# Softmax sums of an attention kernel: folded over 32 partitions on VectorE, finished by narrow matmuls, inverted in 16 columns

## The reference, cut to what matters

```python
x = query                                   # (4, 2048, 512) float32
xn = layernorm(x)                           # over the last axis
q, k, v = heads(xn @ q_w.T + q_b), heads(xn @ k_w.T + k_b), heads(xn @ v_w.T + v_b)   # 16 heads of 32
attn = softmax(q @ k.T / sqrt(32))          # 2048 x 2048 a head, 4 x 16 heads
y = tanh(xn @ weight @ aux1 @ aux2 + bias)
out = x + (attn @ v) @ out_w.T + out_b + y
```

## Time and profile before

| | us |
|---|---|
| median of 3 runs | 4175.6 (4172.01 to 4176.85) |
| span of the profiled execution | 4167.9 |
| PE, POOL, DVE, ACT busy | 4078.0, 3253.1, 3127.0, 2356.4 |
| issue of the merge to its landing, median | 10.4 |

### The profile page before, as it was taken

The page is one execution under the profiler, slowest core; times in us unless marked ns, Lnnn a source line. Parts: engine busy times, 40 slices in busy tenths (PEclk is TensorE's granted clock), DMA queues, the critical chain, the costliest instruction groups (busy, mean ns, idle before and its releaser), DMA issues.

```text
span 4167.9 us, 77711 instructions
## 1 busy us (share of the span) xinstructions
PE 4078.0 (98%) x21216; PEld 2490.3 (60%) x21216; DVE 3127.0 (75%) x5058; ACT 2356.4 (57%) x4515; POOL 3253.1 (78%) x1180
## 2 busy tenths in 40 slices
PE   8999999889999999999999999999999999999999
PEld 6888888645555555555555555555555555555467
DVE  4443334668888888888888888888888888888454
ACT  2221222157676666666676666666666767666621
POOL 1222222179999999999999999999999999999930
PEclk9999999999999999999999999999999999999999
DMA  4444445368878888888888888878888888888787
GB/s 169 162 161 160 151 160 166 122 141 174 172 165 176 176 175 176 171 172 175 173 174 178 177 170 173 171 168 175 176 177 173 175 172 171 176 176 174 154 260 263
DMA packets 246352, 722.11 MB, mean 173 GB/s; under 512 B 87392, under 2 KB 88416, under 8 KB 184544
## 3 DMA queue, kind: packets, MB, share of 16 engines
q0 software_dynamic: 55296, 402.68, 49.8%
q1 hardware_dynamic: 107648, 201.88, 14.2%
q10 hardware_dynamic: 83040, 113.01, 9.8%
HBM read 178.00 MB, written 136.31 MB: 75 GB/s over the span
## 4 chain that ended last, share of the span: by engine, by line
PE 53%; DMA 14%; issue 7%; ACT 3%; POOL 2%; ACTq 0%; POOLq 0%; SPq 0%; DVE 0%; DVEq 0%
PE sm_bank L948 16%; PE st_bank L964 16%; PE pv_bank L970 16%; DMA dma_sum<-pool_sum 10%; DMA dma_sum<-probs 3%; ACT probs L781 3%; PE sm_bank L235 3%; PE sm_bank L970 1%; POOL pool_sum L716 1%; PE st_bank L235 1%; POOL ctx_out L741 0%; DMA q_stack<-s_y 0%; PE sm_bank L957 0%; DMA q_stack<-max_row 0%; POOL dma_sum L727 0%
## 5 line engine op out<-in xcount | busy, mean ns | idle before, releaser
L862 DVE TENSOR_REDUCE part_max<-sm_bank 128x1 f32<-128x512 f32 x4016 | 2442.3, 678 | 412.3 <-PE sm_bank L948 406.0
L716 POOL TENSOR_TENSOR pool_sum<-pool_sum,probs 128x2048 f32<-128x2048 f32 x512 | 2504.9, 4892 | 16.7 <-ACT probs L781 0.9
L781 ACT ACTIVATE probs<-st_bank 128x512 f32<-128x512 f32 x3840 | 1959.4, 616 | 608.6 <-PE st_bank L964 580.6
L964 PE MATMUL st_bank<-q_stack,k_stack 97*128 97x512 f32 x4096 | 1648.4, 403 | 19.2 <-ACT probs L781 8.3
L948 PE MATMUL sm_bank<-k_stack,q_stack 96*128 96x512 f32 x4016 | 1655.1, 412 | 3.0 <-issue 2.7
L948 PEld LDWEIGHTS sm_bank<-k_stack,q_stack 96*128 96x128 f32 x4016 | 763.3, 190 | 550.7 <-DVE part_max L862 334.1
L964 PEld LDWEIGHTS st_bank<-q_stack,k_stack 97*128 97x128 f32 x4096 | 779.9, 191 | 274.8 <-ACT probs L781 128.0
L970 PE MATMUL pv_bank<-probs,v_pair 128*32 128x512 f32 x7680 | 936.0, 602 | 0.0
L970 PEld LDWEIGHTS pv_bank<-probs,v_pair 128*32 128x32 f32 x7680 | 204.9, 110 | 455.7 <-ACT probs L781 262.9
L727 POOL DMA_DIRECT2D dma_sum<-probs x320 | 348.3, 1088 | 70.7 <-ACT probs L781 26.2
L356 POOL TENSOR_TENSOR y_out<-y_out,x_in 128x512 f32<-128x512 f32 x64 | 82.6, 1291 | 406.9 <-ACT y_out L388 401.1
(11 more groups left out here) (100 smaller groups left out, 2431.4 us busy)
## 6 DMA issues: line engine op xcount, KB each, us to landing
dma_sum<-probs POOLq DMA_DIRECT2D x320, 1024.0 KB, 8.3
dma_sum<-pool_sum POOLq DMA_DIRECT2D x64, 1024.0 KB, 10.3
q_stack<-s_q_hi ACTq DMA_DIRECT2D x122, 256.0 KB, 6.6
k_stack<-s_k_hi ACTq DMA_DIRECT2D x122, 256.0 KB, 4.8
x_in<-in_x SPq DMA_DIRECT2D x16, 1024.0 KB, 7.7
s_q_hi<-qk_hi SPq DMA_DIRECT2D x16, 1024.0 KB, 4.3
s_q_lo<-qk_lo SPq DMA_DIRECT2D x16, 1024.0 KB, 6.5
s_k_hi<-qk_hi SPq DMA_DIRECT2D x16, 1024.0 KB, 4.3
```

What stands on the lines that cost most here:

```text
L716: nc.gpsimd.tensor_tensor(total[:], one[:], tile_at(r, kt)[:], ALU.add).then_inc(pool_added, 1)
L781: nc.scalar.activation(tile_at(r, kt)[:, q * BLK:(q + 1) * BLK], st_bank[:, st_place(kt * QB + q)], ACT.Exp, scale=SCALE).then_inc(probs_r ...
L862: nc.vector.tensor_reduce(part_max[:, k:k + 1], sm_bank[:, sm_place(k)], AX.X, ALU.max).then_inc(max_scores_read, 1)
L964: nc.tensor.matmul(st_bank[:, st_place(u)], k_st[r][0:ROWS + 1, kt * P:(kt + 1) * P], q_st[r][0:ROWS + 1, q * BLK:(q + 1) * BLK], start=Tr ...
```

## The change

`dma_sum` (128 x 2048) is no longer the right side of wide matmuls. DVE reduces each quarter of 512 columns: the quarter is seen as 16 blocks of 32 columns, each 32 x 32 block is turned, and the reduction runs over 32 elements, so that partition p of a group of 32 holds the sum over the group's partitions of column p of each block (`fold`, into `folded`, 128 x 64). The folds stand on DVE after maxima units 49, 53, 57 and 61; the first waits for the merge. PE then adds the four groups with a matrix `pick` that has a one where the partition modulo 32 is the output row: four matmuls of 16 columns. The sum's place is after unit 63 (`SUM_UNIT` 64, `CUT` 12). DVE takes the reciprocal of 128 x 16 straight from PSUM ahead of unit 0 (`invert`), which frees the bank, and after unit 3 spreads it to 128 x 512 with a turn of a broadcast (`spread_out`). ACT's copy of the sums is gone. In the last head, with no maxima left, the folds, the inversion and the spreading stand behind DVE's `results(1, 1)`. `pick` is built on POOL at the start with one fill and four selects.

```diff
-SUM_UNIT = 56
-RECIPS = [63, 7, 15]
-CUT = 10
+SUM_UNIT = 64
+FOLDS = [49, 53, 57, 61]
+INVERT, SPREAD = 0, 3
+CUT = 12
...
-        sum_bank, turn_bank = sm_bank[:, sm_place("sum")], sm_bank[0:QT, sm_place("max"), 0:P]
+        sum_bank, turn_bank = sm_bank[:, sm_place("sum"), 0:BLK // DH], sm_bank[0:QT, sm_place("max"), 0:P]
...
-                pool.wait_ge(recip_ready, h * len(RECIPS) + len(RECIPS))
+                pool.wait_ge(recip_ready, h + 1)
...
-                        if kt == CUT - 1:
-                            copy_sums(h, r)
...
-            def recip(h, r, piece):
+            def fold(h, r, piece):
 
                 if piece == 0:
-                    dve.wait_ge(sums_copied, PRIME + h + 1)
-                    dve.wait_ge(context_ready, PRIME + h)
-                cut = [BLK // len(RECIPS) // 8 * 8 * i for i in range(len(RECIPS))] + [BLK]
-                columns = slice(cut[piece], cut[piece + 1])
-                nc.vector.reciprocal(ratio[:, columns], sum_copy[r % 2][:, columns]).then_inc(recip_ready, 1)
+                    dve.wait_ge(joined[r % 2], landed(h, len(CHAINS[0])))
+                total = dma_sum[r % 2][:, piece * BLK:(piece + 1) * BLK]
+                blocks = slice(piece * (BLK // DH), (piece + 1) * (BLK // DH))
+                nc.vector.tensor_reduce(folded[r % 2][:, blocks], total.rearrange("p (b j) -> p b j", j=DH), AX.X,
+                                        ALU.add, apply_transpose=True).then_inc(fold_ready, 1)
+
+            def invert(h):
+                dve.wait_ge(sums_ready, PRIME + h + 1)
+                nc.vector.reciprocal(inverse[:], sum_bank).then_inc(sums_read, 1)
+
+            def spread_out(h):
+                dve.wait_ge(sums_read, PRIME + h + 1)
+                dve.wait_ge(context_ready, PRIME + h)
+                nc.vector.transpose(ratio[:].rearrange("p (b j) -> p b j", j=DH),
+                                    inverse[:].unsqueeze(2).to_broadcast([P, BLK // DH, DH])).then_inc(recip_ready, 1)
...
-                if k in RECIPS and sums_of is not None:
-                    recip(*sums_of, RECIPS.index(k))
+                if sums_of is not None:
+                    if k in FOLDS:
+                        fold(*sums_of, FOLDS.index(k))
+                    if k == SPREAD:
+                        spread_out(sums_of[0])
...
-                    for piece in range(len(RECIPS)):
-                        recip(h, r, piece)
+                    for piece in range(QB):
+                        fold(h, r, piece)
+                    invert(h)
+                    spread_out(h)
...
-                    pe.wait_ge(sums_copied, PRIME + s - 1)
+                    pe.wait_ge(sums_read, PRIME + s - 1 - back)
...
-                pe.wait_ge(joined[r % 2], landed(h, len(CHAINS[0])))
-                spread(sum_bank, ones[:], dma_sum[r % 2], True, True).then_inc(sums_ready, 1)
+                pe.wait_ge(fold_ready, h * QB + QB)
+                width = BLK // DH
+                for q in range(QB):
+                    last = nc.tensor.matmul(sum_bank[q * DH:(q + 1) * DH, :], pick[:],
+                                            folded[r % 2][:, q * width:(q + 1) * width], start=True, stop=True)
+                last.then_inc(sums_ready, 1)
```

More of the change, by code:

```diff
@@ L112, in build_weights @@
         ident_ready, bank_ready, high_ready, bank_free = sem("ident_ready"), sem("bank_ready"), sem("high_ready"), sem("bank_free")
-        small_loaded, wo_stored = sem("small_loaded"), sem("wo_stored")
+        small_loaded, wo_stored, pick_ready = sem("small_loaded"), sem("wo_stored"), sem("pick_ready")
         loaded["x"] = sem("loaded_x")
@@ L147, in _ @@
             nc.gpsimd.memset(keep["ident"][:], 0.0).then_inc(ident_ready, 1)
-            nc.gpsimd.memset(keep["ones"][:], 1.0)
+            nc.gpsimd.memset(keep["pick"][:], 0.0).then_inc(pick_ready, 1)
             nc.gpsimd.memset(keep["power"][:], -0.5)
@@ L152, in _ @@
                                     base=0, pattern=[[-1, P]], channel_multiplier=1).then_inc(ident_ready, 1)
+            for b in range(QB):
+                pool.wait_ge(pick_ready, b + 1)
+                nc.gpsimd.affine_select(out=keep["pick"][:], in_=keep["pick"][:], compare_op=ALU.not_equal, fill=1.0,
+                                        base=-b * DH, pattern=[[-1, DH]], channel_multiplier=1).then_inc(pick_ready, 1)
             pool.wait_ge(var_ready, 1)
@@ L550, in build_attend @@
         dma_sum = [sb(f"dma_sum{s}", [P, SEQ]) for s in range(2)]
-        ones, ident = first["ones"], first["ident"]
+        pick, ident = first["pick"], first["ident"]
         part_max, row_max = first["part_max"], first["row_max"]
@@ L554, in build_attend @@
         pv_copy = [sb(f"pv_copy{s}", [P, BLK]) for s in range(2)]
-        sum_copy = [sb(f"sum_copy{s}", [P, BLK]) for s in range(2)]
+        folded = [sb(f"folded{s}", [P, SEQ // DH]) for s in range(2)]
+        inverse = sb("inverse", [P, BLK // DH])
         ratio = sb("ratio", [P, BLK])
@@ L570, in build_attend @@
         pool_added, sums_ready, recip_ready, context_ready = sem("pool_added"), sem("sums_ready"), sem("recip_ready"), sem("context_ready")
-        pv_copied, sums_copied = sem("pv_copied"), sem("sums_copied")
+        pv_copied, fold_ready, sums_read = sem("pv_copied"), sem("fold_ready"), sem("sums_read")
         context_stored = [sem("context_stored0"), sem("context_stored1")]
@@ L765, in _ @@
         def _(act):
-            for s in (probs_ready, pv_copied, sums_copied):
+            for s in (probs_ready, pv_copied):
                 act.sem_inc(s, PRIME)
@@ L783, in exps, with copy_pv @@
                                          scale=SCALE).then_inc(probs_ready, 1)
-            def copy_bank(h, r, bank, copies, ready, value, copied):
-                act.wait_ge(ready, value)
+            def copy_pv(h, r):
+                act.wait_ge(tile_used, PRIME + h * KT + KT)
                 act.wait_ge(context_ready, PRIME + h - 1)
[L788 to L794, removed]
+                nc.scalar.activation(pv_copy[r % 2][:], pv_bank[:], ACT.Copy).then_inc(pv_copied, 1)
             def high(n, par):
@@ L840, in _ @@
             dve.sem_inc(row_max_ready, PRIME + 1)
+            dve.sem_inc(sums_read, PRIME)
             def negate(s):
@@ L845, in negate @@
                                         ALU.mult).then_inc(max_row_ready, 1)
-            def recip(h, r, piece):
+            def fold(h, r, piece):
                 if piece == 0:
-                    dve.wait_ge(sums_copied, PRIME + h + 1)
-                    dve.wait_ge(context_ready, PRIME + h)
-                cut = [BLK // len(RECIPS) // 8 * 8 * i for i in range(len(RECIPS))] + [BLK]
-                columns = slice(cut[piece], cut[piece + 1])
-                nc.vector.reciprocal(ratio[:, columns], sum_copy[r % 2][:, columns]).then_inc(recip_ready, 1)
+                    dve.wait_ge(joined[r % 2], landed(h, len(CHAINS[0])))
[11 more added lines that the diff above has]
+                                    inverse[:].unsqueeze(2).to_broadcast([P, BLK // DH, DH])).then_inc(recip_ready, 1)
             def maxima(s, k, units, sums_of):
+                if sums_of is not None and k == INVERT:
+                    invert(sums_of[0])
                 if units:
@@ L1067, in build_program @@
             "part_max": sb("part_max", [P, UNITS]), "row_max": sb("row_max", [P, QT]),
-            "ident": sb("ident", [P, P]), "ones": sb("ones", [P, DH]),
+            "ident": sb("ident", [P, P]), "pick": sb("pick", [P, DH]),
             "q_stack1": sb("q_stack1", [P, SEQ], F32R), "k_stack1": sb("k_stack1", [P, SEQ], F32R),
@@ L1073, in build_program @@
         keep = {
-            "ident": first["ident"], "ones": first["ones"], "power": sb("power", [P, JT]),
+            "ident": first["ident"], "pick": first["pick"], "power": sb("power", [P, JT]),
             "qk_bias": sb("qk_bias", [P, 2, CT]), "row_bias": sb("row_bias", [P, 3, DIM]),
```

## The result

The changed kernel takes 4292.9 us (median; 4280.0 to 4302.9) against 4173.8 for the kernel before in the same comparison: ratio 1.0276, 95% interval 1.0257 to 1.0295. The forecast was 4245, with a range of 4170 to 4345. The direction and the place were right. The loss of 119 us is 1.7 times the 70 us (4245 - 4175.6) that were worked out.

The account below looks back on a forecast made before the run. POOL was taken to set the pace, with PE only tenths of a microsecond ahead. Span 4167.9 + 65 (heads) + 4.4 (end) = 4237.3; runs' median 7.7 above the profile's span: 4245 us, range 4170 to 4345.

Parts of the forecast that it names:

- Prices: New operations on DVE and PE: fold 0.61 us, narrow matmuls 0.25, small reciprocal 0.3, transpose 0.6.
- Rival C: On DVE, a fold makes two passes, 1.2 us: 4394 us; chance with its neighbours, over 4345, 0.08.
- The place: DVE waits for the merge after unit 49, PE stops at unit 54, POOL then waits before a head's first join.
- The stop at +1.35: PE starts unit 54 1.35 us after the merge lands, behind a fold of 0.61 and unit 50's 0.68.
- PE's saving worth nothing while POOL sets the pace: Attention stage: work taken from PE alone, 0.8 us a head, turns into idleness before the next merge.
- 78%: POOL's busy share of the whole span, read from the page with POOL taken to run only in the attention stage.
- The loop of 49.8 us: Attention stage, merge landing to landing: 49.8 us a head against 48.74, +1.05; +65 us over 62 heads.
- PE's way from unit 54 to the end of the pair: PE's stretch from 2047.65 to 2050.55 in the kernel before, taken as 2.9 us of the shift.
- the merge's landing: Last term of the head's loop: the merge lands 10.4 us after its issue, the median before the change.
- Evenness: Folds and first joins: DVE idle 1 to 2 us at a head's first fold, POOL about 1 us before its first join.
- The end: Last head: PE's sum waits for folds behind DVE's four results, so PE resumes the output 4.4 us later.
- Rival A: Attention stage: POOL stays the pace, loop 48.7 us, as PE makes up 1 us of the shift; 4180 us, chance 0.14.

Follow-up runs that it names:

- The wait alone: Kernel before, with only a DVE wait for the merge added after unit 49: 4283.3 us, ratio 1.0251.
- the quarter sum: Kernel before, with one quarter of the sum's matmuls and the other three left out: 4182.7 us, ratio 1.0031.
- The repeats: Changed kernel, with eight idle repeats of a score block on PE in front of unit 54: 4257.9 us, ratio 1.0204.
- late folds: Changed kernel, with the folds after units 56, 58, 60 and 62 instead of 49, 53, 57 and 61: 4197.0 us, ratio 1.0048.

## Why the prediction was right or wrong

- Prices: right. Fold 0.61 by step in the forecast, and from 2145.17 to the next instruction 2145.80 it is 0.63; narrow matmuls 0.25 and 0.23; inversion 0.3 and 0.25; transpose 0.6 and 0.7. Rival C, two passes, falls. The Trainium skill (Vector Engine (DVE) Microarchitecture Reference, "The reshape front-end and per-opcode configuration") has the turning array pass one element per cycle per lane. The trace agrees: the turned reduction takes 698 ns where the plain one of as many elements takes 679.
- The place: right. The wait for the merge moved to DVE, stopped PE at unit 54, and the shift reached POOL at the first join. The wait alone makes 107 us. (The stop at +1.35 was added from 0.61 and 0.68, which give 1.29; 1.34 was measured. And the wait moved 2.9 us forward in PE's program, not four: the 4.0 between 2047.65 and 2051.64 hold 1.05 of idleness.)
- PE's saving worth nothing while POOL sets the pace: right, shown by the quarter sum. One reading on the way was wrong: POOL does not run only in the attention stage, it is busy for 190 us in the first 860, so in attention it is nearer its limit than 78% (1960 of 2000 us between 1500 and 3500). This strengthens the argument.
- The loop of 49.8 us: the mis-sized term. The forecast took PE's way from unit 54 to the end of the pair as 2.9 us; in the head read it takes 2095.28 to 2100.92, 5.6 us, since PE works at half speed after its stand. That is 2.7 of the 3.0 us by which the matmuls on tile 0 are later than forecast. The prediction never asked what a stand of 2 to 3 us does to PE's clock. A second term went the other way: the merge's landing was taken as 10.4 us and is 9.3 in the median (8.5 to 10.7). So two errors cancel in part, and a third, below, is that only every other head is a long one. What comes out is 50.68 instead of 49.8, 0.9 us a head. The repeats give back 35 us of the 49 us by which the loss was forecast too low, and the estimate from heads with and without a fall of the clock gives 30 to 50; how much of the 49 is the clock's is known no better.
- Evenness: wrong. The forecast had each head with 1 to 2 us at the fold and about 1 us at the join. The averages are not far from this (49.5 / 39 = 1.3 and 61.8 / 39 = 1.6 us), but heads alternate between the two waits.
- The end: +4.4 forecast, +4.5 measured. (Rival C's 4394 leaves out that its four slower folds would lengthen the end too, by 2.4 us; nothing hangs on it.)
- Rival A (the shift fits POOL's slack): not for this kernel. With the first fold at 51 or later most of the shift fits (POOL waits for PE 5.5 us in 41 heads at 51), and what stays is mostly other waits of POOL, for landings and exponentials (24.3 and 31.3 us).

## What to carry to other kernels

Before a wait is moved to another engine, put the time at which the event comes beside the time at which that engine reaches the wait, and follow the in-order queue behind it; here 16 columns instead of 512 saved 0.8 us of an engine that had nothing to gain, and the wait cost 1.9 us a head. Where two engines are in step by tenths of a microsecond, look for the slack of the next dependency round the loop, and price a stand of the matmul engine with the clock that it loses. Where the transfers are as busy as here (83% before), their order matters: moving one load by one tile gained 0.2%, more than the new arithmetic at any of its places, and moving several lost 1.3% in the kernel before and 3.9% with late folds, which lose 0.5% by themselves.

## What the runs showed of the hardware

- The granted clock of TensorE fell to 1.2 GHz around a stand of 2.87 us in a stage in which PE is over 95% busy (482 of 500 us), and the `use` of a pair of tiles then took 3.64 us instead of 1.92. It did so after 17 of 20 such stands.
- A periodic program can settle into a pattern of two heads, long and short (51.9 and 49.35 us in the mean): a stand of PE, a late first join, and a merge that lands in 8.6 us instead of 9.9. The fall of the clock lengthens the long heads, but two of the long heads had none. Averages over the stage hide it.
- The reduction over turned 32x32 blocks took 698 ns for 128x512, against 679 for the plain one from PSUM, and the transpose of a broadcast 702 ns.
